# Routed feed-forward stage: the first element's routing cut in three, row statistics ahead of two residual sums, the last down products in four banks

## What is computed

```python
x = x + xattn0(ctx, layernorm(x)); x = x + ternary_ffn(layernorm(x)); x = x + xattn1(layernorm(x), ctx)
xf = layernorm(x).reshape(4096, 512)
scores = softmax(xf @ w_gate.T)                  # 8 experts in 4 groups
s = scores + expert_bias                         # best 2 groups by the sum of their 2 scores
masked = where(group kept, s, -inf)              # best 2 experts within them
weights = scores[chosen]
h = silu(rows @ w1[e]) * (rows @ w3[e]); routed = h @ w2[e]
shared = silu(xf @ sw1.T) * (xf @ sw3.T) @ sw2.T # for every token
out = x + shared.at[flat_idx].add(routed)
```

## Time and profile before

| | us |
|---|---|
| median of three runs | 1930.35 (1928.9 to 1932.52) |
| profiled execution, its own time | 1930.36 |
| its span, first to last instruction | 1928.6 |
| routed phase, first product to the end of the span | 1575.1 to 1928.6 |
| mean granted TensorE clock | 0.996 of full speed |

### The profile page before, as it was taken

One profiled execution on the slowest core, in us unless ns is written; L12 is line 12 of the kernel. 1 busy time (PEld: TensorE's weight loads), 2 busy tenths in 40 slices (PEclk: granted clock), 3 DMA queues, 4 the chain that ended last, 5 costly groups with the idle time before them and its releaser, 6 DMA issues.

```text
span 1928.6 us, 42677 instructions
## 1 busy us (share of the span) xinstructions
PE 1884.3 (98%) x13700; PEld 1446.0 (75%) x13700; DVE 1284.5 (67%) x3985; ACT 1032.7 (54%) x2674; POOL 798.1 (41%) x1482
## 2 busy tenths in 40 slices
PE   6999999999999999999999999999999989999998
PEld 5888888888888644444448888888888867787875
DVE  5887876767667678888865665656556566444475
ACT  5777767777777644644445544444454443222252
POOL 3454555656555545655543221322223133222264
PEclk9999999999999999999999999999999999999999
DMA  7343434443342767756552222121221236221131
GB/s 236 124 142 135 139 107 159 146 134 136 134 162 86 147 156 191 181 129 149 129 142 105 79 80 87 55 96 69 88 77 63 102 115 207 94 88 65 66 131 45
DMA packets 221532, 230.32 MB, mean 119 GB/s; under 512 B 123440, under 2 KB 139824, under 8 KB 221376
## 3 DMA queue, kind: packets, MB, share of 16 engines
q1 hardware_dynamic: 221376, 228.42, 38.7%
HBM read 144.47 MB, written 56.64 MB: 104 GB/s over the span
## 4 chain that ended last, share of the span: by engine, by line
PE 91%; DVE 3%; SPq 2%; DMA 2%; ACT 1%; issue 1%; POOL 0%; DVEq 0%; POOLq 0%; ACTq 0%
PE bank L1172 19%; PE bank L1158 18%; PE bank L2698 13%; PE bank L1868 10%; PE bank L1228 8%; PE bank L1243 6%; PE bank L1211 5%; PE bank L1913 5%; PE bank L1148 2%; DMA b_hqT<-b_hq 1%; SPq L1450 1%; PE bank L2601 1%; SPq L1456 1%; PE bank L2737 1%; DVE m_hrow L2532 0%
## 5 line engine op out<-in xcount | busy, mean ns | idle before, releaser
L582 POOL TENSOR_SCALAR a_probs<-a_probs,a_rinv 128x256 f32<-128x256 f32 x512 | 237.5, 483 | 270.1 <-DVE a_rinv L933 270.1
L711 ACT ACTIVATE a_probs<-a_probs,a_negm 128x256 f32<-128x256 f32 x512 | 254.7, 502 | 96.4 <-DVE a_negm L917 95.3
L582 POOL TENSOR_SCALAR c_probs<-c_probs,c_rinv 128x256 f32<-128x256 f32 x128 | 67.1, 534 | 371.8 <-DVE c_rinv L933 371.8
L917 DVE CUSTOM_DVE_ANT_0 a_probs<-bank,a_mbias 128x256 f32<-128x256 f32 x512 | 191.6, 416 | 7.5 <-PE bank L1211 6.8
L2698 PE MATMUL bank<-m_xnT,m_s 128*128 128x512 f32 x768 | 184.9, 392 | 2.7 <-DVE m_hid L2436 2.7
L926 DVE COPY a_pT<-bank 128x512 f32<-128x512 f32 x128 | 88.2, 689 | 135.8 <-PE bank L1228 135.6
L2698 PEld LDWEIGHTS bank<-m_xnT,m_s 128*128 128x128 f32 x768 | 142.8, 188 | 33.5 <-DVE m_hid L2436 3.1
L711 ACT ACTIVATE c_probs<-c_probs,c_negm 128x256 f32<-128x256 f32 x256 | 127.0, 500 | 75.0 <-DVE c_negm L917 75.0
L1228 PE MATMUL bank<-a_ident,a_probs 128*128 128x128 f32 x1024 | 154.8, 274 | 4.0 <-ACT a_pT L719 2.3
L1228 PEld LDWEIGHTS bank<-a_ident,a_probs 128*128 128x128 f32 x1024 | 121.9, 141 | 23.6 <-issue 10.8
L1730 ACT ACTIVATE b_hq<-b_hround 128x1024 bf16<-128x1024 f32 x64 | 67.2, 1052 | 124.2 <-POOL b_hround L1669 119.4
(11 more groups left out here) (287 smaller groups left out, 4323.1 us busy)
## 6 DMA issues: line engine op xcount, KB each, us to landing
kept<-a_cT SPq DMA_DIRECT2D x32, 512.0 KB, 5.4
m_ew<-in_L_ffn_w_dram SPq DMA_DIRECT2D x24, 512.0 KB, 8.7
a_cbuf<-in_ctx_dram SPq DMA_DIRECT2D x16, 512.0 KB, 5.5
a_xbuf<-in_x_dram SPq DMA_DIRECT2D x16, 512.0 KB, 4.7
a_resb<-in_x_dram SPq DMA_DIRECT2D x16, 512.0 KB, 4.1
b_part<-in_L_ffn_w_gate_dram SPq DMA_DIRECT2D x32, 256.0 KB, 2.9
b_part<-in_L_ffn_w_up_dram SPq DMA_DIRECT2D x32, 256.0 KB, 3.7
b_part<-in_L_ffn_w_down_dram SPq DMA_DIRECT2D x32, 256.0 KB, 4.2
```

What stands on the lines that cost most here:

```text
L582: last = nc.gpsimd.tensor_scalar(pr, pr, rinv[:, s, r:r + 1], 0.0, ALU.mult, ALU.add)
L711: nc.scalar.activation(pr, pr, ACT.Exp, bias=negm[:, s, h % 2, t:t + 1], scale=-1.0, accum_out=ssum[:, s, QT * (h % 2) + t:QT * (h % 2) + ...
L917: nc.vector.tensor_tensor_reduce(out=probs[:, s, h % 2, t], in0=s_bank[h][:, t * SEQ:(t + 1) * SEQ], in1=mbias[:, el.par], scale=-sm_scale ...
```

## The change

Five edits, all in the routed phase.

1. `row_stats` of element 1 moves from the start of `m`'s vector program to the end of `vector_behind`, ahead of `c`'s last two residual sums.
2. `route` is cut into `route_scores`, `route_groups` and `route_experts`. In the first iteration DVE runs element 0's scores before the four `lo_x`, its groups (and then `row_stats` of element 2) after `hidden(0, 0)`, its experts after `hidden(0, 1)`; element 1's scores and groups after `hidden(0, 2)`, its experts after `hidden(0, 3)`. Later iterations are as before.
3. ACT takes the exponentials of element 0 right after its first silu, ahead of the four `hi_x`.
4. In the last iteration DVE does end 0 ahead of the `rows_out` of half 23.
5. The last element's four down products go into `g_bank`, `u_bank`, `z_bank`, `g_bank`, with waits for what each bank held; the fold moves from behind half 28 to behind half 27.

```diff
--- before.py
+++ after.py
@@ -2074,7 +2074,7 @@
         return z_bank if number(g) == 0 else t_bank[0]
 
     LOOP_FROM = 4
-    END_TURN, END_DOWN, END_FOLD = 23, 25, 28
+    END_TURN, END_DOWN, END_FOLD = 23, 25, 27
 
     def last_order():
 
@@ -2089,6 +2089,10 @@
 
     def is_step(i):
         return 0 <= i < STEPS
+
+    def down_bank(g, t):
+
+        return (g_bank, u_bank, z_bank, g_bank)[t] if number(g) == LAST else z_bank
 
     def load_raw(sp, n, w):
         view = w.rearrange("(t p) c -> p t c", p=P)
@@ -2353,13 +2357,16 @@
                         nc.scalar.activation(fourths[:], ab_bank[0][:], ACT.Copy).then_inc(fourths_out, 1)
                 return
             silu(g, 0)
+            if number(g) == 0:
+                exponents(g)
             for t in range(TILES):
                 hi_x(act, g.plus(1), t)
             hi_h(g, 0)
             silu(g, 1)
             logits_out(g.plus(1))
             hi_h(g, 1)
-            exponents(g if number(g) == 0 else g.plus(1))
+            if number(g) != 0:
+                exponents(g.plus(1))
             for f in (2, 3):
                 silu(g, f)
                 hi_h(g, f)
@@ -2423,6 +2430,7 @@
             ins = nc.vector.tensor_copy(xT_first[:, :, at:at + EXPERTS],
                                         t_bank[0][:].rearrange("p (k n) -> p k n", k=KC)[:, :, 0:EXPERTS])
         ins.then_inc(first_ready, 1)
+        row_stats(dve, first[1])
 
     def vector(dve):
         V = nc.vector
@@ -2438,7 +2446,7 @@
         def rows_out(g, t):
             dve.wait_ge(r_loaded[t // 2], g.n * 16 + 16)
             dve.wait_ge(z_done, g.n * TILES + t + 1)
-            V.tensor_tensor(resb[:, t], z_bank[:], resb[:, t], ALU.add).then_inc(out_done, 1)
+            V.tensor_tensor(resb[:, t], down_bank(g, t)[:], resb[:, t], ALU.add).then_inc(out_done, 1)
             if number(g) == 0 and t == 0:
                 dve.wait_ge(out_done, 1)
                 V.tensor_copy(first_out[:], resb[0:EXPERTS, 0]).then_inc(first_ready, 1)
@@ -2450,6 +2458,9 @@
 
         def over_experts(ap):
             return ap.unsqueeze(2).broadcast_to([P, ap.shape[1], EXPERTS])
+
+        def by_group(t):
+            return t[:].rearrange("p t (g a) -> p t g a", a=2)
 
         def by_choice(ap):
             return ap.unsqueeze(2).broadcast_to(tc)
@@ -2464,14 +2475,22 @@
 
         def route(g):
 
+            route_scores(g)
+            route_groups(g)
+            route_experts(g)
+
+        def route_scores(g):
+
             count[0] = 0
-            of_group = bass.ds(g.n * TILES, TILES)
             dve.wait_ge(lg_done, g.n + 1)
             V.tensor_reduce(lg[:], lg_bank(g)[:, 0:TILES * 64].rearrange("p (t b r) -> p t r b", t=TILES, b=2)[:, :, 0:EXPERTS],
                             AX.X, ALU.add).then_inc(lg_read, 1)
             dve.wait_ge(lg_read, g.n + 1)
             step(g, V.reduce_max(top[:], lg[:], AX.X))
             V.tensor_tensor(expo[:], lg[:], over_experts(top[:]), ALU.subtract).then_inc(shifted, 1)
+
+        def route_groups(g):
+
             dve.wait_ge(exp_ready, g.n + 1)
             step(g, V.reduce_sum(total[:], expo[:], AX.X))
             step(g, V.reciprocal(inverse[:], total[:]))
@@ -2479,13 +2498,17 @@
             dve.wait_ge(bias_loaded, 16)
             step(g, V.tensor_tensor(score[:], prob[:], bias_row[:].unsqueeze(1).broadcast_to(te), ALU.add))
 
-            halves = score[:].rearrange("p t (g a) -> p t g a", a=2)
+            halves = by_group(score)
             step(g, V.tensor_tensor(gscore[:], halves[:, :, :, 0], halves[:, :, :, 1], ALU.add))
             dve.wait_ge(consts_ready, CONSTS)
             ranks(g, grank[:], gscore[:], group_first[:], GROUPS)
             step(g, V.tensor_scalar(gkeep[:], grank[:], 1.5, None, ALU.is_lt))
             step(g, V.tensor_scalar(gdrop[:], gkeep[:], -1.0, BIG, ALU.add, ALU.mult))
-            mp = masked[:].rearrange("p t (g a) -> p t g a", a=2)
+
+        def route_experts(g):
+
+            of_group = bass.ds(g.n * TILES, TILES)
+            halves, mp = by_group(score), by_group(masked)
             for a in range(2):
                 ins = V.tensor_tensor(mp[:, :, :, a], halves[:, :, :, a], gkeep[:], ALU.mult)
             step(g, ins)
@@ -2545,8 +2568,6 @@
                 dve.wait_ge(y_done, 1)
                 V.tensor_tensor(first_out[:], ab_bank[1][0:EXPERTS, :], first_out[:], ALU.add).then_inc(first_done, 1)
 
-        row_stats(dve, first[1])
-
         def iteration(g):
             if number(g) == LAST:
                 for u, i, half in last_order():
@@ -2558,23 +2579,37 @@
                     elif u == "up" and half == 1:
                         hidden(g, i)
                     elif u == "down before" and half == 1:
+                        if i == TILES - 1:
+                            end(0)
                         rows_out(g.plus(-1), i)
                     elif u == "down" and half == 1:
                         rows_out(g, i)
-                    elif u == "end":
+                    elif u == "end" and i > 0:
                         end(i)
                 return
+            if number(g) == 0:
+                route_scores(g)
             for t in range(TILES):
                 lo_x(dve, g.plus(1), t)
             for f in range(KC):
                 hidden(g, f)
+                if number(g) == 0:
+                    if f == 0:
+                        route_groups(g)
+                        row_stats(dve, g.plus(2))
+                    elif f == 1:
+                        route_experts(g)
+                    elif f == 2:
+                        route_scores(g.plus(1))
+                        route_groups(g.plus(1))
+                    else:
+                        route_experts(g.plus(1))
+                    continue
                 if has_before(g):
                     rows_out(g.plus(-1), f)
                 if f == 0 and g.has(2):
                     row_stats(dve, g.plus(2))
                 if f == 1:
-                    route(g if number(g) == 0 else g.plus(1))
-                elif f == 2 and number(g) == 0:
                     route(g.plus(1))
             if before_last(g):
                 runs()
@@ -2686,11 +2721,17 @@
             product(u_bank, lambda a, b, k: (sw[1][:, b, k, f * P:(f + 1) * P], xnT[g.par][:, a, k]), ks, u_done)
 
         def down(g, t, ks):
-            if ks[0] == 0:
+            if ks[0] == 0 and number(g) != LAST:
                 wait_for(pe, out_done, g.n * TILES + t)
+            elif ks[0] == 0 and t == 0:
+                pe.wait_ge(silu_done, groups * KC)
+            elif ks[0] == 0 and t == 1:
+                pe.wait_ge(h_done, groups * KC)
+            elif ks[0] == 0:
+                pe.wait_ge(out_done, LAST * TILES + t - 2)
             if t == 0:
                 pe.wait_ge(h_lo, g.n * KC + ks[-1] + 1)
-            product(z_bank, lambda a, b, k: (hidT[g.par][:, a, k, t * P:(t + 1) * P], sw[2][:, b, k]), ks, z_done)
+            product(down_bank(g, t), lambda a, b, k: (hidT[g.par][:, a, k, t * P:(t + 1) * P], sw[2][:, b, k]), ks, z_done)
 
         def product(bank, operands, ks, done):
             for k in ks:
```

## The result

The changed kernel took 1918.54 us, the median of four runs (1915.71 to 1920.42), against 1930.36 before (1928.9 to 1932.52). The ratio is 0.9937, 95% interval 0.9919 to 0.9954: 11.8 us less, where 11.5 were forecast.

A forecast was written before the change was run, and what follows sets the result against it. TensorE, busy for 98% of the span, was taken as the bound, so gains come only from idle stretches or slow matmuls: 3.7 + 3.2 + 4.6 = 11.5 off 1930.4 gives 1918.9 us, range 1916.4 to 1923.6.

The forecast's parts named there:

- Part 1: First iteration, earlier row statistics: element 1's turning starts without its 2.00 us wait and runs faster; 3.7 us gained.
- Part 2: First iteration, routing in parts: the 2.70 us stall ahead of `up(0, 3)` goes, with its slower product; 3.2 us gained.
- Part 3: Last element's end: sums earlier and down products in separate banks remove TensorE's waits for DVE; 4.6 us gained.
- Rival B: Element 1's turning: the run of 20 transposes lowers the clock, 1.7 us back, 1920.6 us; chance 0.09.
- Rival C: A late `hidden` in the first iteration or another wait at the end: 2 to 4 us back; chance 0.12.
- Rival D: DVE bounds the first iteration, 0.47 us per routing step beside POOL, at most 27; up to 1938 us; chance 0.02.
- Rival E: No change: an unseen dependence in the first iteration and final stores binding the end; 1927 to 1930 us; chance 0.05.

The follow-up runs named there:

- e1: Kernel before with only element 1's row statistics moved ahead of the last two residual sums: 1927.17 us, ratio 0.9983.
- e2: Kernel before with only the routing cut in parts and element 0's exponentials taken earlier on ACT: 1928.13 us, ratio 0.9981.
- e3: Kernel before with only the two edits of the end (end 0 earlier; down products in separate banks, fold earlier): 1925.79 us, ratio 0.9976.
- e5: Kernel before with only end 0 ahead of the last residual sum of the element before: end stretch 25.60 us, against 26.92.
- e8: Changed kernel with 8 more bn_stats on DVE ahead of element 2's statistics: first logits to expert rows 18.24 us, 2.05 more.
- e6: Kernel before with only the last down products in separate banks and the fold behind half 27: end stretch 24.69 us, against 26.92.
- e4: Changed kernel with DVE's sum of the expert counts moved right behind the last routing: 1916.05 us, 0.9927 of the kernel before.
- e7: Changed kernel with element 1's 16 transposes made three times over: first product to first logits 14.01 us, against 10.52.
- e12: Same kernel as e4, timed again beside e11 on one chip: 1916.05 us, 0.9918 of the kernel before.
- e10: Changed kernel with the fold behind half 28 again: end stretch 22.34 us, against 22.33.
- e9: Changed kernel with ACT's exponential of element 0 behind the four copies: 10.52 us to first logits, 16.19 on to expert rows, both unchanged.
- e11: Changed kernel itself, timed again beside e12 and the kernel before on one chip: 1919.00 us, ratio 0.9932.

## Why the prediction was right

**The sum.** Forecast 11.5, measured 11.32 in the profiles compared and 11.8 in the medians. By terms: 3.7 against 3.70, 3.2 against 2.98, 4.6 against 4.59.

**Part 1.** The reading that the turning was paced by POOL's tiles and the low clock, so that more than the 2.00 of idle time would go, is what e1 shows (10.51). The term holds a part that is not the edit's own: 0.72 of it is the low clock, which that place has in some executions only. At full clock the edit is worth 2.98. Against the first stretch of e2 or e3 the changed kernel would have shown 2.98, against that of e5 4.40, so that 3.7 met 3.70 so closely is in part luck of the execution compared. The residual sums moved back and nothing waited for them. The weight loads started 4.57 behind the first product instead of 8.41 (1576.43 and 1583.55 less the starts 1571.86 and 1575.14), 3.84 earlier.

**Part 2.** The stall went (e2), and the layout of DVE held. Taking off the 3.28 by which this execution was ahead, `hidden(0, 0)` was to end at 1580.9 and the statistics of element 2 at 1586.4. DVE's rows:

```profile
1579.92 0.69 DVE L2444 TENSOR_TENSOR m_hid<-bank,m_act_gate 128x512 f32<-128x512 f32 x1
...
1581.62 1.16 DVE L2471 TENSOR_TENSOR m_group_first<-m_gscore 128x12 f32<-128x12 f32 x1
...
1586.44 0.38 DVE L2389 BATCH_NORM_AGGREGATE m_mv<-m_stats 128x2 f32<-128x6 f32 x4
```

They ended at 1580.61 and 1586.82. The mis-sized term is the 0.22 added for the product that starts without a stall (2.72 instead of 2.94). It did not come: the four products ahead of the expert rows take 1598.57 - 1587.44 = 11.13, 0.25 more than 4 x 2.72, so this quarter of a microsecond was not the restart behind the stall: it is there without one. The margin of 2 to 2.5 was 2.8 (e8).

**Part 3.** Right in its sum and in what each new wait costs (e3, e5, e6). One number under it was wrong: `hsum` was to take 1.30 and be ready 1.45 behind the product's start.

```profile
1891.87 0.42 DVE L2562 COPY m_hsum<-bank 128x256 f32<-128x256 f32 x1 [0.16 <-PE bank L2778]
1892.33 0.42 DVE L2564 TENSOR_TENSOR m_hsum<-bank,m_hsum 128x256 f32<-128x256 f32 x1
1892.79 1.31 DVE L2566 TENSOR_TENSOR m_hsum<-m_hsum,m_factor 128x256 f32<-128x256 f32 x1
```

It took 2.23 and was ready at 1894.10, 0.3 before TensorE wanted it. The step that takes 1.31 here took 0.42 before; it is the only one of the three with both operands in SBUF, and it now lies beside POOL's `lo_h` of the last hidden product. The gain is whole by 0.3 us.

**Rival B (the clock).** Did not happen: no execution of the changed kernel or of its variants (eight profiles, e4 and e7 to e12 among them) has a granted clock below full between the first product and the last. By the rule taken from the Trainium skill ("TensorE: Matmul & The Clock Gate", section "PE-mode transpose"), transposes do not count as activity as products do; the one execution of e7, with 5.6 us of f32 transposes at a granted clock of 1.00, did not bear this out. For transposes with pauses between them the rule is not refuted. Just ahead of the routed phase such transposes (1542.25 to 1550.20 in e12) have idle stretches of 0.41, 0.88 and 0.99 between them. Behind them the granted clock was 0.50 in e5, e7 and e12 (1550 to 1553 in e12) and full in the other eleven profiles, and no run separates the pauses from the transposes. The price of 1.7 fits a low stretch filled with products (1.78 in e1, 1.72 in e2, 1.56 in e5); at the place that rival B is about, the low clock cost 0.72, 0.89 and 1.42 (before, e6, e5).

**Rival C** was 2.8 us away in the first iteration and 0.3 away at the end.

**Rival D (DVE the bound).** Its price was built on the wrong mechanism, 0.47 for every step beside POOL. The rows say otherwise. DVE and POOL in the changed kernel:

```profile
1581.42 1.32 POOL L2229 TENSOR_TENSOR m_hidT<-m_hid,m_hidT 128x512 fp32r<-128x512 f32 x1 [3.21 <-ACT m_hidT L2310]
1581.62 1.16 DVE L2471 TENSOR_TENSOR m_group_first<-m_gscore 128x12 f32<-128x12 f32 x1
...
1588.73 1.33 POOL L2229 TENSOR_TENSOR m_hidT<-m_hid,m_hidT 128x512 fp32r<-128x512 f32 x1 [5.99 <-ACT m_hidT L2310]
1588.81 1.30 DVE L2471 TENSOR_TENSOR m_expert_first<-m_masked 128x20 f32<-128x20 f32 x1
...
1600.43 1.31 POOL L2229 TENSOR_TENSOR m_hidT<-m_hid,m_hidT 128x512 fp32r<-128x512 f32 x1 [3.55 <-ACT m_hidT L2310]
1600.51 1.28 DVE L2471 TENSOR_TENSOR m_expert_first<-m_masked 128x20 f32<-128x20 f32 x1
```

One compare step each time ends within 0.05 us of POOL's instruction, and the steps behind it are as fast as ever. So, as far as these rows go, one POOL instruction costs DVE at most its own 1.3 us, once, however many steps there are. This is the exclusive lock, held for the full instruction, of which the Trainium skill ("SBUF — State Buffer", section "Terms") tells, and the trace agrees. The kernel before fits: its four slow steps, from 1599.79 to 1602.62, stand beside four tiles of `xn` (1599.46 to 1602.59). From the first product to `up(1, 0)` (1571.86 to 1606.68) POOL is busy for 15.74 us in all, so the bound is about 16 us and not 27; by this D could not have made the kernel slower, as it decides from 19.5 on. No run put more POOL work there to try it.

**Rival E** fell: e3's final stores did not bind, as the 4.53 that its end gained (26.92 to 22.39) shows.

## What to carry to other kernels

On an engine that is busy for 98% of the span, list its brackets of idle time and cost each by when the next piece could start, restarts and pace of the producer included; such gains added up here, where each wait stood at another time. When one engine serves both the long chain (a routing) and the short step that the bound engine needs next, cut the chain to the length of a product and put each part directly behind a short step. When two waits stand behind one another at the same place (the sum and the bank), remove both: here 1.04 of the 4.59 came only with both edits.

## What the runs showed of the hardware

**An idle stretch of 2.0 to 2.9 us costs more than itself in some executions.** The six profiled kernels that still had idle stretches of 2 us or more (before, e1, e2, e3, e5, e6) have fourteen of them in the routed phase, and six times the granted clock was 0.50 behind one: once in before, e1, e2 and e6, twice in e5, never in e3. The eight without such stretches (the longest is 1.72, in e8) show no low clock in that phase. One low stretch cost 1.56, 1.72 and 1.78 us (e5, e2, e1) where products stood in it, and 0.72 to 1.4 where POOL paced part of it (first stretch of 14.22 in before, 14.39 in e6, 14.92 in e5, against 13.50). Shorter pauses are not safe everywhere, as those of at most 0.99 between the transposes ahead of the routed phase show (rival B). The same place is hit in one execution and not in the next, which e1 (hit at the second stall) and before (at the first) show.

**The low clock goes with part of the spread.** The mean granted clock is between 0.994 and 0.999 in the runs of this case. Of the 25 runs of the kernel before beside e1 to e4, the 16 at 0.996 took 1931.2 on average, the four at 0.995 took 1935.1, the three at 0.997 took 1929.7. In the profiles it shows ahead of the routed phase: where 1.7 us were lost there at the low clock (six profiles), the first product started at 1570.0 to 1574.1, where 6.8 were lost (e10, e12) at 1577.1 and 1576.9. A single time of this kernel thus says little on a change of 1 us, while the routed phase read from its first product repeats within 0.1 us (342.14, 342.21, 342.20 and 342.12 in the changed kernel, e9, e10 and e11).
